# Local-attention tiles: GpSimd's sum of an even tile waits for a softmax normalisation, and the band mask is added by four quarter-array products

## The reference

```python
for l in range(DEPTH):                       # DEPTH = 2
    h = shift_token(x)
    q, k, v = split(h @ wqkv, 3)             # 8 heads of 64
    q, k = rotary_xpos(l2norm(q) * qs, l2norm(k) * ksc)
    sim  = q_window @ k_window.T             # window of 64, look back one window
    sim  = where((i < j) | (i > j + 64), -big, sim)
    x = x + (softmax(sim) @ v) @ wo
    h = layernorm(shift_token(x)) * lg + lb
    a, g = split(h @ w1 + b1, 2)
    x = x + (a * gelu(g)) @ w2 + b2
```

## Time and profile before

| | |
|---|---|
| time, median of 3 runs | 407.36 us (407.35 to 408.51) |
| the profiled execution | 407.63 us, of which its span is 405.6 us |
| busy share of the span | PE 87%, DVE 82%, ACT 74%, POOL 15% |
| chain that ended last | PE 43%, DVE 27%, ACT 18%, issue 10% |
| granted TensorE clock, mean | 0.979 |
| stretch of tiles 0 to 15 | about 204 us to the end |

### The profile page before, as it was taken

The page is one execution under the profiler, slowest core; times in us unless marked ns, Lnnn a source line. Parts: engine busy times, 40 slices in busy tenths (PEclk is TensorE's granted clock), DMA queues, the critical chain, the costliest instruction groups (busy, mean ns, idle before and its releaser), DMA issues.

```text
span 405.6 us, 10259 instructions
## 1 busy us (share of the span) xinstructions
PE 353.1 (87%) x4047; PEld 252.6 (62%) x4051; DVE 333.5 (82%) x716; ACT 301.1 (74%) x732; POOL 61.1 (15%) x48
## 2 busy tenths in 40 slices
PE   2899999998967688998698889899999999998676
PEld 1498888887742334555455556576667767676565
DVE  4989987896477989979689999989898999995433
ACT  1689999896375427776757878898989898986563
POOL 2000002000203021000033033204032323221110
PEclk9999999999989989999999999999999999999869
DMA  8800010000000000000000000000000000000000
GB/s 309 354 4 3 4 42 3 3 4 3 2 0 2 0 1 2 0 2 2 0 2 2 1 2 1 2 0 2 1 2 2 1 2 2 1 2 0 2 27 26
DMA packets 1774, 8.29 MB, mean 20 GB/s; under 512 B 192, under 2 KB 448, under 8 KB 1472
## 3 DMA queue, kind: packets, MB, share of 16 engines
q1 hardware_dynamic: 1728, 7.65, 4.8%
HBM read 7.12 MB, written 0.52 MB: 19 GB/s over the span
## 4 chain that ended last, share of the span: by engine, by line
PE 43%; DVE 27%; ACT 18%; issue 10%; DMA 1%; DVEq 0%; ACTq 0%
PE ps L250 16%; ACT PT L1529 5%; ACT blk L1409 3%; DVE PT L1225 3%; DVE lneg L1209 3%; PE ps L511 3%; PE ps L625 3%; DVE blk L1183 2%; PE ps L661 2%; DVE ss_floor L1193 2%; ACT PT L1599 2%; PE ps L377 2%; PE ps L498 2%; PE ps L587 2%; PE ps L615 2%
## 5 line engine op out<-in xcount | busy, mean ns | idle before, releaser
L1733 POOL TENSOR_TENSOR blk<-blk 128x1024 f32<-128x1024 f32 x16 | 37.8, 2360 | 169.1 <-DVE blk L1187 169.1
L1529 ACT ACTIVATE PT<-ps,lneg 128x128 f32<-128x128 f32 x128 | 45.2, 379 | 5.3 <-DVE lneg L1209 5.3
L573 PE MATMUL ps<-w_f,full 128*128 128x512 f32 x96 | 47.3, 609 | 0.9 <-issue 0.9
L250 PEld LDWEIGHTS ps<-blk,st 128*128 128x128 bf16 x768 | 26.8, 98 | 3.8
L1043 DVE TENSOR_REDUCE mneg<-ps 128x4 bf16<-128x512 bf16 x32 | 22.0, 688 | 8.2 <-PE ps L355 7.9
L1529 ACT ACTIVATION_READ_ACCUMULATOR PT<-ps,lneg 128x1 f32 x128 | 28.0, 219 | 0.0
L250 PE MATMUL ps<-blk,rel 128*128 128x64 bf16 x768 | 27.6, 193 | 0.0
L250 PE MATMUL ps<-blk,st 128*128 128x64 bf16 x768 | 27.6, 193 | 0.0
L1586 ACT ACTIVATE PT<-ps 128x512 f32<-128x512 f32 x32 | 17.4, 594 | 12.9 <-PE ps L511 12.9
L1209 DVE TENSOR_REDUCE lneg<-ps 128x8 f32<-128x1024 f32 x16 | 19.6, 1223 | 8.6 <-PE ps L250 8.5
L1225 DVE TENSOR_TENSOR PT<-PT,lrec 128x512 f32<-128x512 f32 x32 | 25.3, 790 | 1.1
(11 more groups left out here) (234 smaller groups left out, 911.7 us busy)
## 6 DMA issues: line engine op xcount, KB each, us to landing
w_f<-f_dram SPq DMA_DIRECT2D x2, 1689.0 KB, 13.4
w_x<-l_dram SPq DMA_DIRECT2D x1, 774.0 KB, 6.1
w_f<-ffn_dram SPq DMA_DIRECT2D x1, 561.0 KB, 8.1
X<-x_dram SPq DMA_DIRECT2D x1, 512.0 KB, 3.7
ctxT<-ctxT_dram SPq DMA_DIRECT2D x1, 512.0 KB, 4.6
OT<-maskT_dram SPq DMA_DIRECT2D x1, 512.0 KB, 7.2
rest<-l_dram SPq DMA_DIRECT2D x1, 385.0 KB, 4.8
const<-const_dram SPq DMA_DIRECT2D x1, 324.0 KB, 6.4
```

The lines of the kernel that those rows point to most:

```text
L250: return mm(out, l, r, start=start, stop=False, skip_group_check=True)
L573: m = mm(ps[:, c, :], hT[:, n, :], w_f[:, l, F_QKV + 512 * c:F_QKV + 512 * (c + 1)], start=True, stop=True)
L1529: e = a(S1[:, i % 2, P * k:P * (k + 1)], ps[:, 3 + c, P * j:P * (j + 1)], ACT.Exp, bias=lneg[:, i % 2, k:k + 1], accum_out=lsum[:, i % 2, ...
L1733: g_.tensor_tensor(R[:, i % 2, :], R[:, i % 2, :], T2, ALU.add).then_inc(sem("pair_sum"), 1)
```

## The change

The GpSimd sum for an even tile i from 6 on gets a second wait: the normalisation of tile i - 2 must have ended, in both halves. The band was added by one product of the full 128x128 array for each of the two banks; now each bank takes two products of 64x64 quarters of the array (64 rows in, 64 partitions out), four in all, and every one of the four uses another quarter. Each has 512 columns, as before. For that a second band with its row halves swapped comes with the constants (128 more columns of 776), and DVE makes one more cast near the start.

```diff
-C_IDENT, C_SHIFT, C_BAND, C_ROWMASK, C_ROT, C_END = 0, 128, 256, 384, 392, 392 + 256
+C_IDENT, C_SHIFT, C_BAND, C_ROWMASK, C_ROT, C_BANDX, C_END = 0, 128, 256, 384, 392, 648, 648 + 128
@@ constants()
+    c[:, C_BANDX:C_BANDX + P] = np.roll(c[:, C_BAND:C_BAND + P], 64, 0)
@@ build()
-        band_b = sb("band_b", [P], BF16)
+        band_b = sb("band_b", [2, P], BF16)
@@ score_band(i)
                 for c in range(2):
-                    add(ps[:, 3 + c, :], ident_b[:, :],
-                        band_b[:, :].rearrange("p (o k) -> p o k", o=1).to_broadcast([P, 4, P]), start=True)
+                    for s in range(2):
+                        d, r = 64 * s, 64 * ((s + c) % 2)
+                        add(ps[d:d + 64, 3 + c, :], ident_b[r:r + 64, r:r + 64],
+                            band_b[r:r + 64, c, :].rearrange("p (o k) -> p o k", o=1).to_broadcast([64, 4, P]), start=True)
@@ DVE
-            v.tensor_copy(band_b[:, :], const[:, C_BAND:C_BAND + P]).then_inc(sem("consts_b"), 1)
+            step(v.tensor_copy(band_b[:, 0, :], const[:, C_BAND:C_BAND + P]))
+            v.tensor_copy(band_b[:, 1, :], const[:, C_BANDX:C_BANDX + P]).then_inc(sem("consts_b"), 1)
@@ GpSimd
             def sum_pairs(i):
                 pool.wait_ge(sem("rotated"), i + 1)
+                if i >= 6 and i % 2 == 0:
+                    pool.wait_ge(sem("p_norm"), 2 * (i - 2) + 2)
                 g_.tensor_tensor(R[:, i % 2, :], R[:, i % 2, :], T2, ALU.add).then_inc(sem("pair_sum"), 1)
```

## The result

The changed kernel takes 403.97 us (median of 20 runs; one of them, at 675.83 us, was disturbed, the other 19 took 402.31 to 406.63 and have the median 403.83), the kernel before 407.43 us in the same series (20 runs, 405.22 to 409.17). The medians lie 3.46 us apart, 0.85%. The ratio, estimated from all undisturbed runs of both and not the quotient of the medians, is 0.9937 with a 95% interval of 0.9919 to 0.9955: 0.63% or 2.6 us less.

What follows compares the result with a forecast made beforehand. It took DVE's wait on GpSimd's sum in even tiles as the bound, ACT next. Wait -1.3, band +0.15, cast +0.14 gave -1.0 on 407.63: 406.6, less 0.27 for the runs' median, 406.4 us; range 404.9 to 409.8.

Steps and rivals of the forecast that it cites:

- The stall on GpSimd: In five even tiles DVE's second normalisation half stood still 0.62 us until GpSimd's sum ended; the wait removes it.
- ACT as the cap: In each of five pairs, ACT's gapless chain lets the exponentials gain only 0.26 us of 0.7 offered.
- The term of -1.3: Gain from the wait on GpSimd over five tiles, 5 x 0.26 = 1.3 us less.
- late for `unit_norm`: GpSimd's delayed sum would end at 309.9, with 0.4 us to spare before `unit_norm` needs it.
- The stopped DVE: Rival: the late sum holds DVE's gatings until GpSimd ends; five pairs lose 6 us, 412; chance 0.04.
- The band: PE's four quarter products run together, 0.21 us of stream; with shape changes counted, +0.15 us in sum.
- the rivals of two, three and four streams: Quarters of one bank exclude each other: 408.1, 409.8, 411.5; chance 0.10 for two, 0.18 for three or four.
- The loss of 0.15 us in tile 13: In tiles 13 and 14 PE doesn't wait, so the band costs 0.58 against 0.43: 0.15 lost each.
- In front of heads: Bands there already paid the shape change out: 0.05 us won each, two or three on the chain.
- +0.15: Sum of the band's gains and losses over all tiles, in us added to the time.
- The casts: Near the start, one more DVE cast on the chain, ahead of the one ACT waits for: +0.14 us.
- The end falls otherwise on the clock: Around 381.5 to 385.0 us, earlier work may meet another half-clock division: 1 us either way, on every case.

Runs made afterwards that it cites:

- e7: Changed kernel with ACT's `head_root(i + 2)` moved behind the second table load of a round: 403.37 us, ratio 0.9910 to the kernel before.
- e8: Kernel before with ACT's `head_root(i + 2)` moved behind the second table load of a round: 406.86 us, ratio 0.9999 to the kernel before.
- e1: Kernel before with only the added wait of GpSimd's even sums, band and constants unchanged: 404.41 us, ratio 0.9943.
- e2: Changed kernel without the added wait, so only the four-quarter band with its cast and constants: 406.92 us, ratio 0.9996.
- e3: Kernel before with only the extra cast and larger constants, old band and sums: 407.91 us, ratio 1.0021.
- e4: The changed kernel run again, unaltered, in a later series: 404.01 us, ratio 0.9947 to the kernel before.
- e5: Kernel before with 29 unread products in PE's pauses of the last two tiles: 403.48 us, ratio 0.9921.
- e6: Changed kernel with 29 unread products in PE's pauses of the last two tiles: 402.39 us, ratio 0.9893 to the kernel before.
- e10: Changed kernel with seven useless DVE statistics on the chain of tile 0's start: 406.08 us, ratio 0.9976 to the kernel before.
- e11: Kernel before with seven useless DVE statistics on the chain of tile 0's start: 406.38 us, ratio 0.9993.

## Why the prediction was wrong, step by step

**The stall on GpSimd: right.** Its 0.62 us are gone from all five tiles (L1229: 692 ns mean over 32, before 790). The transposes start at 306.78, the heads at 307.79, the maximum at 309.00, the exponentials at 310.61. That is 0.2 to 0.3 us ahead of the steps' times, as is the whole pair in this profile (its first band at 294.06, before 294.35).

**ACT as the cap, 0.26 us of 0.7 offered: right.** A round of 22.13 us against the 22.14 forecast, no idle before the exponentials, and e7 against e8. The term of -1.3 measured -1.36 in e1. The sum was not late for `unit_norm`, 0.49 us to spare for 0.4 forecast.

**The stopped DVE: did not come** (its 412 was also added up too low: a maximum 1.2 us later than before in five pairs gives 407.4 + 6 = 413.4). The gatings now lie inside GpSimd's sum and take what they took before, 470 to 484 ns; their line in the changed kernel is (ns min/median/max, first and last start):

```profile
L1236 DVE SCALAR_TENSOR_TENSOR PT<-ps,w_f,PT x24: 470/476/485, 263.4 to 397.9; 128x256 f32<-128x256 f32 x16, 85x256 f32<-85x256 f32 x8
```

**The band: the mechanism right, its term mis-sized.** The four products start within 0.01 us of each other, two of them into each bank, and the next product follows 0.34 us behind the first (316.19 to 316.53), 0.43 before. So quarters of one bank don't exclude each other, and the rivals of two, three and four streams are out. By the rule of the Trainium skill that the prediction cites ("TensorEngine Tiling (Array Packing)", "Restrictions and Gotchas") they would have; the trace doesn't agree, and the measurement decides. The loss of 0.15 us in tile 13 was set too high. PE's timeline of the changed kernel there, and of the kernel before:

```profile
359.32 1.06 PE L588 MATMUL ps<-const,blk 128*128 128x128 f32 x8 [0.18 <-ACT full L1518]
...
362.61 1.16 PE L251 MATMUL ps<-blk 64*128 64x128 f32 x16
```

```profile
360.43 1.06 PE L587 MATMUL ps<-const,blk 128*128 128x128 f32 x8 [0.40 <-ACT full L1514]
...
363.69 1.16 PE L250 MATMUL ps<-blk 64*128 64x128 f32 x16
```

With the band between them, the heads follow the transposes by 3.29 us instead of 3.26: 0.03 lost. Tile 14 can't tell, since its band fell into half clock in the changed kernel. In front of heads 0.12 were won over the four bands of tiles 0 to 3 together (38.98 us from 211.59 to 250.57; before, 39.10 from 211.10 to 250.20). Instead of +0.15 the whole band comes to about 0 (-0.01 in e2, before the end).

**The casts: as said** (two of 0.14 us on the chain; start us, us). In the time, e3 can't resolve them.

```profile
10.43 0.14 DVE band_b L1001
10.56 0.14 DVE band_b L1002
```

**"The end falls otherwise on the clock": this step failed.** It was written as 1 us either way, with a mean of zero, and so was left out of the sum. Both were wrong. The work came out 1.5 us shorter (1.51 in the profiles, 1.5 at equal clock in e4) for 1.0 forecast; 407.4 - 1.5 = 405.9 would have lain inside the range. What carried it out was the clock: on top of the work it gave 0.5 to 1.2 us in e4's series (by means, by medians) and 1.0 to 1.9 by e5 and e6. In the series of the result some 2 of the 3.46 us are left for it, but there the clocks of before's runs are not on record, and its median of 407.43 lies 0.5 to 0.7 us above those of the three later series, so a part is the scatter of before. The profile of before could have warned of the size: the earlier trace rows show one drop, and the second, 6.9 us long behind 388.3, was on no row that the prediction used, though PE worked in 6.21 of it. A sign for the term could not be had from the profile of before; its width could, up to 4.9 us that could be lost or won.

The three runs of before that were shown (407.35 to 408.51) also hid how wide it scatters: in 35 runs of one series it took 403.69 to 408.43, a range as wide as the effect.

**Open:** why the drops fall as they do in one execution and otherwise in the next; whether the changed kernel's smaller loss is a lasting property of its order or of where its end lies (e10 and e11 say the second, not cleanly); and how large its share is, since the ways to read it give 0.5 to 1.9 us.

## What to carry to other kernels

A GpSimd operation on SBUF tensors belongs beside DVE's work with PSUM operands, not beside a DVE instruction with two SBUF inputs; what its move gains is read at the next engine down the chain, here ACT, whose 0.28 us of idle time told the gain within 0.01 us a round. When a profile shows half clock behind a pause of PE, take the whole amount that the drops can cost as the width of the forecast, and give PE unread work in the pauses before judging changes under 1%: it narrowed the spread of the runs from 4.7 us (26 runs) to 1.1 to 2.5 (5 to 12 runs) and won 3.5 us by itself in the kernel before. And compare two kernels at one mean clock, run by run: here it found the change's 1.5 us of work in medians 2.7 us apart.

## What was not expected of the hardware

- Extra matmuls made the kernel faster: 29 unread products in the pauses of the last two tiles, 406.95 to 403.48 us, granted clock 1.00 behind 366 us instead of 0.51 in 10 us of the last 25.
- Two row halves of the array write one PSUM bank side by side: 64x64 quarters with 512 columns start 0.003 us apart (the two full products before: 0.215), all four within 0.010, and the next product follows 0.34 us behind the first.
- 1.6 us of added work on the chain at the start left the time of the kernel before unchanged (406.38 against 406.85, ratio 0.9993, 0.9967 to 1.0019).
